# Two graph-attention layers of a four-layer GNN kernel: another order of the pipeline stages on three engines

## The chip, the cores and the metric

The kernel runs on one core of one Trainium2 chip, in one launch. The time is the device time of that core in microseconds (us); the median of three runs is given, and beside it the time of the one execution that the profiler recorded. The engines are TensorE (PE, its weight loads PEld), VectorE (DVE), ScalarE (ACT), GpSimd (POOL) and SyncE (SP, which only issues DMAs).

## The reference

Four graph layers run one after the other over 100,000 nodes with 64 features and 50,000 edges sorted by target node. Each adds its result to the node features after a layer norm and a ReLU. The first layer is a GATv2 attention with 8 heads of 16 features (followed by a second one with 2 heads of 64), the fourth a GATv2 attention with 4 heads of 16. Per edge both compute:

```python
z = leaky_relu(xl[src] + xr[dst] + ee, 0.2)
score = einsum('ehc,hc->eh', z, att)
m = segment_max(score, dst)
a = exp(score - m[dst])
alpha = a / (segment_sum(a, dst)[dst] + 1e-16)
out = segment_sum(xl[src] * alpha[..., None], dst)
```

The fourth layer also needs the mean and the variance of `out` over the nodes. The other layers are not touched by the change.

## The kernel before

`program` calls one block for each part of the work, and between two blocks all engines meet at a barrier. `gat_block` is called three times: with tag "a" (first attention, R=128 rows, 8 heads), "b" (wide, R=128, 2 heads) and "g" (last attention, R=64, 4 heads). The change touches the tags "a" and "g", the first and the third call. Tiles carry the tag in front (`a_xg`, `g_xg`).

A block works through 98 chunks of 512 edges, and each engine has its own list of stages. A stage is a function for one chunk. The helper `flow` runs step t of an engine as: for each entry (lag, stage) of the list, in the order of the list, run the stage for chunk t minus lag. So the list sets two things: the order of the work on an engine within a step, and how many steps after its gather a chunk meets the stage. Chunks go round four sets of buffers (SL = 4), and semaphores count chunks, so an engine waits only where the data of a chunk, or a buffer, isn't there yet. After a few steps written out, `flow` on DVE, PE and SP (and on ACT for "b" and "g") is a hardware loop whose body holds four steps. POOL's list is written out in full.

The stages, with the lines that are named later:

- POOL `gather` (line 802): eight indirect DMAs for each chunk, 128 rows each, with the row numbers read from `c_at` in SBUF. It waits first until the chunk four before has been normed and stored.
- DVE `norm`: in "g" an addition of two SBUF tiles first (830), then eight row statistics (649) and twelve small steps (661 to 675). `leaky` (850) takes the maximum of z and 0.2 z, the second operand from PSUM. `quotients`: a reciprocal (890) and the product with PSUM (905, in "g" 912). `denominator` (869, "a" only): a running sum along the edges over `ex`, both operands in SBUF. `sums`: the weights times features (879, both operands in SBUF), then the running sum (882, operands in SBUF). `maximum`: a small copy (858), a running maximum with scores from PSUM (859), a subtraction with PSUM (860).
- ACT: `normed` (938, in "a" two copies of node numbers more, 945 and 946; in "g" two stores, 950 and 951), `turned` (959, PSUM to SBUF), `values` (975, 0.2 z), `features` (968), `exponents` (983, 984, 986), `results` (stores the chunk; in "g" also a square, 992).
- PE: `turn` (1035, four transposes of the normed rows), `project` ("a" 1052 to 1054, "g" 1049 and 1050), `scores` (1060), `results` (1069, 1071 for "a": the running sums transposed), `moments` (1076, "g" only).

The chain of one chunk is gather, norm, normed, turn, turned, project, values, leaky, scores, maximum, exponents, sums and denominator, results on PE, quotients, results on ACT, moments.

Of the kernel before, what the change touches and what calls it, by code (L numbers as in the profile page):

```python
# [64 lines left out]
def hold(eng, turn, *waits):  # L65


    for sem, value in waits:
        eng.wait_ge(sem, value)
        eng.sem_inc(turn, 1)  # L70
# [52 lines left out]
def flow(eng, stages, total=NCH, slots=2, looped=True, alike=None):  # L123

    stages = [(s[0], s[1], total if len(s) < 3 else s[2]) for s in stages]
    lag = max(s for s, _, _ in stages)
    first = -(-(lag + slots) // slots) * slots  # L130
    last = (alike or total) // slots * slots
    if not looped:
        first = last = total

    def step(t):
        for s, fn, chunks in stages:
            n = t - s
            if 0 <= n < chunks:
                fn(n, n % slots, n // slots, n >= slots)

    for t in range(first):
        step(t)
    if looped:
        with eng.Fori(first // slots, last // slots) as i:
            for u in range(slots):
                for s, fn, _ in stages:
                    n = i * slots + (u - s)
                    fn(n, (u - s) % slots, i + (u - s) // slots, True)
    for t in range(last, total + lag):
        step(t)  # L150


def later(n, least=1):

    return not isinstance(n, int) or n >= least
# [524 lines left out]
def gat_block(nc, a, T, C, tag, H, R, wide):  # L680
# [10 lines left out]
    with ExitStack() as ctx:  # L691
# [3 lines left out]
        L = 2 if wide else 3  # L695
# [14 lines left out]
        both = R < P  # L710
# [98 lines left out]
        def _(dve):  # L809
# [104 lines left out]
                                    ).then_inc(S["oE"], 1)  # L914
            if wide:
                stages = [(L, leaky), (L + 2, quotients), (L + 1, denominator), (L + 1, sums), (L, maximum)]
            else:
                stages = [(L, leaky), (L + 2, quotients), (L + 1, sums), (L, maximum), (L - 2, norm)]
                if not both:
                    stages.insert(2, (L + 1, denominator))  # L920
            flow(dve, stages, slots=SL)
            if tag == "g":
                dve.wait_ge(S["bs"], NCH)
# [4 lines left out]
        def _(act):  # L928
# [65 lines left out]
                act.dma_start(rows(T[{"a": "H1", "b": "HR"}[tag]], n), oE[k][:, :, :]).then_inc(s_st[k], 16)  # L994
            if wide:
                stages = [(L - 1, features), (L - 2, turned), (L, exponents), (L + 2, results)]
            else:
                stages = [(L, values), (L, features), (L - 1, normed), (L - 1, turned), (L, exponents), (L + 2, results)]
            flow(act, stages, slots=SL, looped=tag != "a")
            for k in slots:  # L1000
                act.wait_ge(s_st[k], 16 * chunks_of(k, SL))
# [14 lines left out]
        @block.tensor  # L1016
        def _(pe):
            mm, tr = nc.tensor.matmul, nc.tensor.transpose
            wz, we, att = ((C["wz1"], C["we1p"], C["att1r"]) if tag == "a" else
                           (None, C["we2p"], C["att2r"]) if tag == "b" else  # L1020
                           (C["wz3"], C["we3"], C["att3r"]))

            def turn(n, k, q, old):
                if wide:
                    pe.wait_ge(s_g[k], NG * (q + 1))
                else:
                    pe.wait_ge(S["hn"], n + 1)
                if later(n):
                    pe.wait_ge(S["h"], n)
                if wide:  # L1030
                    for j in range(J):
                        tr(split(bT2[:, :])[:, :, j], xg[k][:, j, 1, :], C["ident"][:, :])  # L1032
                for j in range(J):
                    src = xg[k][:, j, 0, :] if wide else hn[k][:, j, :, :].rearrange("p s d -> p (s d)")
                    last = tr(split(bT[:, :])[:, :, j], src, C["ident"][:, :])  # L1035
                last.then_inc(S["hT"], 1)

            def project(n, k, q, old):

                pe.wait_ge(s_ext[k], 16 * (q + 1))  # L1040
                pe.wait_ge(S["h"], n + 1)
                if later(n):
                    pe.wait_ge(S["zt"], n)
                    pe.wait_ge(S["xl"], n)
                wx, hx = (C["wl2"][:, :], hT[k][:, :]) if wide else (wz[0:D, :], hT[k][0:D, :])
                wr, hr = (C["wr2"][:, :], hT2[k][:, :]) if wide else (wz[:, :], hT[k][:, :])
                if tag == "g":

                    mm(bZ[:, :], C["wz3"][:, :], hr, start=True, stop=False)
                    mm(bZ[:, :], we[:, :], ext[k][:, :], start=False, stop=True).then_inc(S["z"], 1)  # L1050
                    return
                mm(bZ[0:R, :], wr, hr, start=True, stop=False)
                mm(bZ[0:R, :], we[:, :], ext[k][:, :], start=False, stop=True)
                mm(bX[0:R, :], wx, hx, start=True, stop=True).then_inc(S["z"], 1)

            def scores(n, k, q, old):
                hold(pe, S["pturn"], (S["zt"], n + 1))
                if later(n):
                    hold(pe, S["pturn"], (S["ed"], n))
                mm(bS[:, :], att[:, :], zt[k][:, :], start=True, stop=True).then_inc(S["s"], 1)  # L1060

            def results(n, k, q, old):
                hold(pe, S["pturn"], (S["sum"], n + 1))
                if not both:
                    hold(pe, S["pturn"], (S["den"], n + 1))
                if later(n):
                    hold(pe, S["pturn"], (S["oE"], n))
                for j in range(J):
                    last = tr(bO[:, j * P:(j + 1) * P], split(num[k][:, :])[:, :, j], C["ident"][:, :])
                    if not both:  # L1070
                        last = tr(bD[:, j * P:(j + 1) * P], split(den[k][:, :])[:, :, j], C["ident"][:, :])
                last.then_inc(S["o"], 1)
            def moments(n, k, q, old):
                hold(pe, S["pturn"], (S["sq"], n + 1), (s_em[k], 16 * (q + 1)))
                for j in range(J):
                    last = mm(bB[:, :], oE[k][:, j, :, :].rearrange("p s r -> p (s r)"), em[k][:, j:j + 1],
                              start=isinstance(n, int) and n == 0 and j == 0, stop=isinstance(n, int) and n == NCH - 1 and j == J - 1)
                last.then_inc(S["bs"], 1)
            if wide:
                stages = [(L, scores), (L - 1, project), (L - 2, turn), (L + 1, results)]  # L1080
            else:
                stages = [(L, project), (L, scores), (L - 1, turn), (L + 1, results)]
            if tag == "g":
                stages.append((L + 3, moments))
            flow(pe, stages, slots=SL)


# [1187 lines left out]
```

## Time and profile before

| what | value |
|---|---|
| median of 3 runs | 7306.34 us (7302.04 to 7308.86) |
| profiled execution, its own time | 7280.67 us |
| span of the profile | 7278.9 us |
| busy over the span: DVE, POOL, PE, ACT | 75%, 61%, 55%, 44% |
| "a": first gather starts, last gather starts, last DVE work ends | 654.6, 1716.8, 1751.6 us |
| "g": first gather starts, last gather starts, last DVE work on g_oE | 5561.5, 6600.0, 6630.9 us |
| mean granted TensorE clock | 0.721 of full speed |

Busy shares over the whole span mix twelve blocks with different limits. The two blocks of the change take about 1100 and 1075 us of the 7279, and are read by themselves. In the rows below "idle <-X" behind a group is the time in which the engine stood still before these instructions and what ended it; "issue" is a pause in which it waited for nothing that the profile shows.

### The profile page before, as it was taken

The page shows a single profiled execution, that of the slowest core. Times are in us where ns is not written, and L with a number is a line of the kernel's source. Part 1 is how long each engine was busy: PE and PEld are TensorE (multiplying, and loading weights), DVE is VectorE, ACT ScalarE, POOL GpSimd, SP SyncE. Part 2 cuts the span into 40 slices and gives each one's busy share as a digit, 9 for nine tenths or more (in the row PEclk, how much of TensorE's full clock was granted, in tenths as well). Part 3 has the DMA queues.
Part 4 walks back from the last instruction along what each step waited for, and adds up shares of the span by engine and source line. Part 5 has one row for each costly group of instructions (what it writes and reads, how often), then busy time and mean ns, then how long its engine had stood idle before and what let it go on. Part 6 is the DMA issues. An engine that isn't in the chain of part 4 may idle for free. (4 is left out here: it accounts for less than half of the span.)

```text
span 7278.9 us, 83566 instructions
## 1 busy us (share of the span) xinstructions
PE 3968.5 (55%) x13024; PEld 2369.0 (33%) x13024; DVE 5486.2 (75%) x16937; ACT 3171.6 (44%) x7568; POOL 4455.4 (61%) x4321
## 2 busy tenths in 40 slices
PE   0002666664665665997000989876886766773000
PEld 0000332322333334886000545672332433331000
DVE  4502898986777777887777999776887888886886
ACT  0001666663333333776444000124554666665555
POOL 2777777775777776775776000007664777774776
PEclk9999677776888887555555989558997676665555
DMA  6001555555333332212998000459884555554554
GB/s 190 4 1 34 99 98 98 100 98 81 87 85 84 86 85 61 49 47 57 121 118 102 2 5 1 136 150 129 155 152 108 116 113 115 113 115 110 169 167 136
DMA packets 905930, 687.04 MB, mean 94 GB/s; under 512 B 595425, under 2 KB 744702, under 8 KB 905180
## 3 DMA queue, kind: packets, MB, share of 16 engines
q1 hardware_dynamic: 517168, 403.39, 20.5%
q0 software_dynamic: 137984, 138.92, 18.9%
q10 hardware_dynamic: 250600, 143.02, 6.5%
q14 instruction: 147, 1.20, 0.1%
q8 instruction: 31, 0.51, 0.0%
HBM read 491.06 MB, written 227.24 MB: 99 GB/s over the span
## 5 line engine op out<-in xcount | busy, mean ns | idle before, releaser
L1793 POOL DMA_INDIRECT f_dg<-t_D,c_at x392 | 379.7, 969 | 1132.5 <-POOLq L179 943.3
L802 POOL DMA_INDIRECT b_xg<-t_H,c_at x784 | 828.4, 1057 | 286.0 <-issue 238.6
L802 POOL DMA_INDIRECT g_xg<-t_D,c_at x784 | 801.7, 1023 | 319.9 <-issue 237.7
L802 POOL DMA_INDIRECT a_xg<-t_XL,c_at x784 | 824.6, 1052 | 250.1 <-issue 238.7
L2181 POOL DMA_INDIRECT out<-n_yo,c_at x392 | 430.8, 1099 | 237.5 <-issue 116.0
L440 POOL DMA_INDIRECT t_XL<-su_pos,su_scatx x392 | 388.2, 990 | 244.7 <-DMA t_XL<-in_nodes 125.7
L1326 POOL DMA_INDIRECT l_d<-t_D,l_ix x392 | 399.3, 1019 | 174.8 <-issue 115.8
L1141 POOL DMA_INDIRECT t_RANK<-m_place,m_at x392 | 400.8, 1022 | 160.9 <-issue 115.7
L938 ACT ACTIVATE a_hn<-a_xg,a_sm 128x64 f32<-128x64 f32 x784 | 269.9, 429 | 399.0 <-DVE a_sm L675 398.0
L1375 ACT ACTIVATE l_hn<-l_xs,l_sm 128x64 f32<-128x64 f32 x784 | 265.0, 426 | 284.0 <-DVE l_sm L675 218.9
L2160 ACT ACTIVATE n_h<-n_x,n_sm 128x64 f32<-128x64 f32 (+1 forms) x800 | 269.4, 426 | 210.0 <-DVE n_sm L675 210.0
L1915 ACT ACTIVATE f_hn<-f_xs,f_bykind 128x64 f32<-128x64 f32 x784 | 265.1, 426 | 178.9 <-DVE f_bykind L1825 178.9
L1032 PE MATMUL b_bank<-c_ident,b_xg 128*128 128x128 f32 x392 | 93.6, 383 | 415.4 <-DMA b_xg<-t_H,c_at 415.4
L1060 PE MATMUL a_bank<-a_zt,c_att1r 128*128 128x512 f32 x196 | 196.4, 1105 | 221.2 <-DVE a_zt L850 221.2
L1416 PE MATMUL pr_prow<-c_ident,pr_col 128*1 128x128 f32 x2 | 0.6, 395 | 567.0 <-DVE pr_col L1434 567.0
L1035 PE MATMUL a_bank<-c_ident,a_hn 128*128 128x128 f32 x392 | 108.4, 432 | 369.1 <-ACT a_hn L938 369.0
L938 ACT ACTIVATE g_hn<-g_xg,g_sm 128x64 f32<-128x64 f32 x784 | 269.6, 427 | 76.4 <-DVE g_sm L675 76.2
L1060 PE MATMUL g_bank<-g_zt,c_att3r 128*128 128x512 f32 x196 | 159.5, 907 | 258.2 <-DVE g_zt L850 258.2
L958 ACT ACTIVATE b_hT<-b_bank 128x512 f32<-128x512 f32 x98 | 58.5, 597 | 521.1 <-PE b_bank L1035 521.1
L1253 ACT ACTIVATE m_xn<-m_pa,m_sm 128x64 f32<-128x64 f32 x784 | 242.4, 414 | 90.5 <-DVE m_sm L675 89.1
L1704 ACT ACTIVATE e_ng<-e_pw 128x256 f32<-128x256 f32 x98 | 37.5, 383 | 535.2 <-PE e_pw L1695 535.2
L1495 PE MATMUL pb_sums<-pb_rhs,pb_lhs 128*128 128x392 f32 x784 | 260.6, 496 | 11.3 <-DVE pb_rhs L1486 11.3
(451 smaller groups left out, 13667.4 us busy)
## 6 DMA issues: line engine op xcount, KB each, us to landing
a_ends<-t_LAST SPq DMA_DIRECT2D x98, 256.0 KB
t_XSD<-a_xg SPq DMA_DIRECT2D x98, 256.0 KB
t_H<-a_oE ACTq DMA_DIRECT2D x98, 256.0 KB
b_ends<-t_LAST SPq DMA_DIRECT2D x98, 256.0 KB
l_xb<-t_XSD SPq DMA_DIRECT2D x49, 512.0 KB
f_rl<-t_REL SPq DMA_DIRECT2D x49, 512.0 KB
g_xb<-t_XSD SPq DMA_DIRECT2D x98, 256.0 KB
g_ends<-t_LAST SPq DMA_DIRECT2D x98, 256.0 KB
```

The source lines that it names most:

```text
L440: nc.gpsimd.indirect_dma_start(lp, bass.IndirectOffsetOnAxis(ap=scatx[:, f:f + 1], axis=0), pos[:, f:f + 1].bitcast(F32), None, bounds_che ...
L802: nc.gpsimd.indirect_dma_start(xg[k][:, j, i, :], None, table, bass.IndirectOffsetOnAxis(ap=C["at"][:, i, n * J + j:n * J + j + 1], axis=0 ...
L938: last = f(hn[k][:, g // 2, g % 2, :], xg[k][:, g // 2, g % 2, 0:D], ACT.Relu, bias=sm[:, 5, g:g + 1], scale=sm[:, 4, g:g + 1])
L1060: mm(bS[:, :], att[:, :], zt[k][:, :], start=True, stop=True).then_inc(S["s"], 1)
L1141: nc.gpsimd.indirect_dma_start(rank, bass.IndirectOffsetOnAxis(ap=at[k][:, j:j + 1], axis=0), place[k][:, j:j + 1], None).then_inc(s_rank[ ...
L1326: nc.gpsimd.indirect_dma_start(d1[k][:, 0, j, :], None, T["D1"], bass.IndirectOffsetOnAxis(ap=ix[k][:, j:j + 1], axis=0)).then_inc(s_g[k], 16)
L1375: last = nc.scalar.activation(hn[k][:, g % 2, g // 2, :], xs[k][:, g // 2, g % 2, :], ACT.Relu, bias=sm[:, 5, g:g + 1], scale=sm[:, 4, g:g ...
L1495: nc.tensor.matmul(sums[:, :], lhs[c % SL][:, :], rhs[c % SL][:, :], start=(c == 0), stop=(c == EF - 1)).then_inc(s_mm, 1)
L1793: nc.gpsimd.indirect_dma_start(dg[k][:, u, j, :], None, T["D2"], bass.IndirectOffsetOnAxis(ap=C["at"][:, 0, (2 * n + u) * J + j:(2 * n + u ...
L1915: last = f(hn[k][:, g // J, g % J, c, :], xs[k][:, g // J, g % J, :], ACT.Relu, bias=by_kind[:, c, 1, g:g + 1], scale=by_kind[:, c, 0, g:g ...
L2160: last = f(h[k][0:np_, g, :], x[k][0:np_, g, :], ACT.Relu, bias=sm[0:np_, 5, g:g + 1], scale=sm[0:np_, 4, g:g + 1])
L2181: nc.gpsimd.indirect_dma_start(out, bass.IndirectOffsetOnAxis(ap=C["at"][:, 0, j:j + 1], axis=0), yo[:, j, :], None, bounds_check=N - 1, o ...
```

## The change

The lists of stages for "a" and "g" get another order, and some lags change. No instruction is added, removed or given another size; "b" keeps its lists.

```diff
 # DVE
+            elif tag == "a":
+                stages = [(4, denominator), (3, leaky), (4, sums), (5, quotients), (3, maximum), (1, norm)]
             else:
-                stages = [(L, leaky), (L + 2, quotients), (L + 1, sums), (L, maximum), (L - 2, norm)]
-                if not both:
-                    stages.insert(2, (L + 1, denominator))
+                stages = [(1, norm), (3, leaky), (5, quotients), (4, sums), (3, maximum)]
 # ACT
+            elif tag == "a":
+                stages = [(3, values), (2, normed), (3, features), (2, turned), (3, exponents), (5, results)]
             else:
-                stages = [(L, values), (L, features), (L - 1, normed), (L - 1, turned), (L, exponents), (L + 2, results)]
+                stages = [(3, values), (3, features), (2, turned), (1, normed), (3, exponents), (6, results)]
 # PE
+            elif tag == "a":
+                stages = [(3, project), (5, results), (3, scores), (2, turn)]
             else:
-                stages = [(L, project), (L, scores), (L - 1, turn), (L + 1, results)]
-            if tag == "g":
-                stages.append((L + 3, moments))
+                stages = [(2, turn), (7, moments), (3, scores), (2, project), (4, results)]
```

L is 3 for both tags. In "a" the lags of DVE stay as they were, `denominator` goes from just ahead of `sums` to the head of the step, and `leaky` and `sums` follow it ahead of `quotients`; PE's `results` goes from the end of the step (lag 4) to between `project` and `scores` (lag 5). In "g" DVE's `norm` goes from the end of a step to its head; ACT takes `normed` one step sooner and behind `turned`, and stores one step later; PE takes `project` one step sooner and behind `scores`, and `moments` one step later.

## Rows read from the trace of the kernel before

**Rows 1.** Groups on POOL in the two blocks: busy us, mean ns, idle before

```profile
L802 POOL DMA_INDIRECT a_xg<-t_XL,c_at x784 | 824.6, 1052 | 250.1 <-issue 238.7 <-POOLq L179 11.5
L802 POOL DMA_INDIRECT g_xg<-t_D,c_at x784 | 801.7, 1023 | 319.9 <-issue 237.7 <-POOLq L179 81.3 <-DMA t_HN<-g_hn 0.9
```

**Rows 2.** Tile a_xg: ns min/median/max, first and last start

```profile
L802 POOL DMA_INDIRECT a_xg<-t_XL,c_at x784: 940/944/1781, 654.6 to 1716.8; - x196
```

**Rows 3.** Waits of DVE, 700 to 1700 us and 5620 to 6580 us: total, times, longest

```profile
DVE a_zt L850 <- ACT a_zt L975: 38.2, 39, 1.8
DVE a_bn L649 <- DMA a_xg<-t_XL,c_at: 9.3, 35, 1.4
...
DVE g_xg L830 <- DMA g_xg<-t_D,c_at: 75.3, 83, 1.6
```

**Rows 4.** Timeline of POOL in "a" around 1005 us: start, duration

```profile
999.57 1.60 POOL L802 DMA_INDIRECT a_xg<-t_XL,c_at  x1 [0.30 <-issue]
...
1008.97 0.94 POOL L802 DMA_INDIRECT a_xg<-t_XL,c_at  x1 [0.30 <-issue]
1010.22 1.55 POOL L802 DMA_INDIRECT a_xg<-t_XL,c_at  x1 [0.30 <-issue]
```

**Rows 5.** Timeline of DVE over the same time

```profile
1002.64 1.11 DVE L649 BATCH_NORM_STATS2 a_bn<-a_xg 128x6 f32<-128x64 f32 x8
...
1006.10 0.68 DVE L850 TENSOR_TENSOR a_zt<-a_zt,a_bank 128x512 f32<-128x512 f32 x1
1006.70 0.35 DVE L890 RECIPROCAL a_recT<-a_bank 128x32 f32<-128x32 f32 x1
...
1007.79 1.27 DVE L869 TENSOR_TENSOR_SCAN a_den<-a_ex,a_den 128x512 f32<-128x512 f32 x1
1008.98 0.71 DVE L879 TENSOR_TENSOR a_msg<-a_ex,a_xl 128x512 f32<-128x512 f32 x1
1009.73 1.28 DVE L882 TENSOR_TENSOR_SCAN a_num<-a_ex,a_num,a_msg 128x512 f32<-128x512 f32 x1
...
1012.41 0.69 DVE L860 TENSOR_TENSOR a_ed<-a_bank,a_r 128x512 f32<-128x512 f32 x1
```

**Rows 6.** Timeline of DVE in "a", a step with the loop's turn in it

```profile
1035.21 0.69 DVE L860 TENSOR_TENSOR a_ed<-a_bank,a_r 128x512 f32<-128x512 f32 x1
1035.82 1.10 DVE L649 BATCH_NORM_STATS2 a_bn<-a_xg 128x6 f32<-128x64 f32 x8
...
1039.59 0.69 DVE L850 TENSOR_TENSOR a_zt<-a_zt,a_bank 128x512 f32<-128x512 f32 x1 [0.33 <-issue]
```

**Rows 7.** Timeline of POOL and DVE in "g" around 5890 us

```profile
5886.65 1.43 POOL L802 DMA_INDIRECT g_xg<-t_D,c_at  x1 [0.30 <-issue]
...
5893.37 1.89 POOL L802 DMA_INDIRECT g_xg<-t_D,c_at  x1 [0.30 <-issue]
...
5886.57 0.69 DVE L830 TENSOR_TENSOR g_xg<-g_xg,g_xb 128x512 f32<-128x512 f32 x1 [1.39 <-DMA g_xg<-t_D,c_at]
...
5892.43 0.67 DVE L879 TENSOR_TENSOR g_ex<-g_ex,g_xl 64x512 f32<-64x512 f32 x1
5893.23 1.28 DVE L882 TENSOR_TENSOR_SCAN g_num<-g_ex,g_num 128x512 f32<-128x512 f32 x1
```

**Rows 8.** Timeline of all engines in "a", 1209 to 1217 us

```profile
1209.29 0.69 DVE L860 TENSOR_TENSOR a_ed<-a_bank,a_r 128x512 f32<-128x512 f32 x1
...
1210.65 1.12 PE L1054 MATMUL a_bank<-a_hT,c_wz 64*128 64x512 f32 x2
...
1211.20 1.06 ACT L986 ACTIVATE a_ex<-a_gap 128x1024 f32<-128x1024 f32 x1
...
1214.64 2.05 PE L1060 MATMUL a_bank<-a_zt,c_att1r 128*128 128x512 f32 x2 [2.87 <-DVE a_zt L850]
```

**Rows 9.** Timeline of the end of "g": the last chunk's addition and its quotients

```profile
6603.71 0.69 DVE L830 TENSOR_TENSOR g_xg<-g_xg,g_xb 128x512 f32<-128x512 f32 x1 [0.51 <-DMA g_xg<-t_D,c_at]
...
6630.88 0.42 DVE L912 TENSOR_TENSOR g_oE<-g_bank,g_recT 128x256 f32<-128x256 f32 x1
```

## The prediction

> **What bounds the kernel now.** I read first the groups on POOL in each of the two blocks. In both, POOL issues 784 gathers, and outside the wait at the start of the block nothing but a fixed pause stands between them: 238.7 us over 783 pauses, 0.305 us each, put down to "issue" [rows 1]. It is hardly ever held back by its own waits (0.9 us in all of "g"). So the end of a block is set by the rate of the gathers. The median gather takes 0.944 us [rows 2]; with the pause that is 1.248 us, and eight make 9.98 us for a chunk. But the first and the last gather of "a" lie 1062.2 us apart [rows 2], over 783 steps 1.357 us, or 10.85 us for a chunk. The mean gather is 1.052 us, not 0.944 [rows 1]: 0.87 us a chunk are lost in stretched gathers (85 us over the block). In "g" the mean is 1.023: 0.63 us a chunk, 62 us in all, and 10.61 us for a chunk.
>
> Next I laid the timelines of POOL and DVE side by side to see what stretches a gather. In "a" the gather that starts at 1010.22 takes 1.55 us and ends at 1011.77 [rows 4]. It began 0.49 us into the running sum of line 882, which ends at 1011.01 [rows 5], so it ends 0.76 us behind that. In "g" the gather at 5893.37 begins 0.14 us into the same sum, takes 1.89 us and ends 0.75 us behind it; the one at 5886.65 begins 0.08 us into the addition of line 830 and ends 0.82 us behind it [rows 7]. The gather at 1008.97 starts 0.01 us ahead of the product of line 879 and takes its normal 0.94 us [rows 4, 5]. All the long gathers of both blocks fit one rule, where "two SBUF operands" are lines 830, 869, 879 and 882: a gather that starts from about 0.1 us after the start of such an instruction is held until that instruction is over, and ends 0.75 us (running sum) or 0.82 us (product, addition) behind it. As an undisturbed one takes 0.944, starts later than 1.09 us into a running sum (1.28 + 0.75 - 0.944), or 0.55 us into a product, cost nothing. The running maximum of line 859, with one operand in PSUM, stretches none.
>
> The Trainium skill, SBUF — State Buffer, section Who interferes with whom, has a GpSimd instruction and a DVE instruction with two SBUF inputs share a port, with whichever starts first holding it for its whole length; it adds, as inferred only, that a tensor_tensor takes the reading side while descriptor generation needs the writing side, so that it wouldn't hold up a DMA's issue. The trace speaks against that addition: the addition of line 830 holds a gather by 0.49 us. By that addition lines 830 and 879 would cost nothing and the sum for "g" would lose one of its two causes; I go by the rows.
>
> Last I asked how far DVE is from being the bound. In "a" it waits for a gather's landing only 35 times in 92 chunks, 9.3 us in all, and 38.2 us for ACT's `values` ahead of `leaky`; in "g" it waits for the landing in 83 of about 90 chunks, 75.3 us [rows 3]. Without any wait a step of DVE in "a" is: norm 3.46 (1002.64 to 1006.10), leaky 0.60, reciprocal and product 1.09, line 869 1.19, product 0.75, line 882 to the start of 860 2.68 [rows 5], and from 860 to the next norm 0.61 [rows 6]: 10.38 us. The same sum with the shorter gaps seen elsewhere in the block is some 10.2. One step in four holds the turn of the loop, which shows ahead of the first stage of a list: norm to `leaky` is then 3.77 and not 3.3 to 3.5 [rows 6], +0.1 us a chunk. So DVE needs about 10.35 us, more than POOL's undisturbed 9.98 and less than the 10.85 that it takes. "a" is bound by POOL, and by how often DVE's stages catch its gathers.
>
> **"a": the new order, walked through.** No work goes; the cost of every moved instruction is unchanged, and the DMAs that ACT and SP issue are the same in number. What changes is the distance between DVE's three instructions that catch gathers.
>
> Before, 869, 879 and 882 follow each other at 0, 1.19 and 1.94 us [rows 5]. A gather caught by 869 is released at 1.27, ends at 2.03, and the next starts at 2.33: 0.39 into 882, held 0.70 us more. So each catch costs twice, u plus 0.7, where u is what remained of 869.
>
> After, 869 is at 0, `leaky` at 1.19, the product at 1.79 and the sum of 882 at about 2.5. The gather behind a caught one again starts at 2.33: 0.54 into the product, where the window has just closed; it costs 0.01. Released or not, the next starts at 3.58, 1.09 into the running sum, where the window has closed too. The second catch is gone, and with it 0.7 us of the chunks that had it. A gather that starts between 1.09 and 1.25 us into 869 costs nothing at all.
>
> Now the steady state has two forms. **Form 1, DVE waits for the landing.** A chunk's last gather ends at E (1001.17 [rows 4]) and norm starts at E + 1.47 [rows 5]; line 869 follows 3.43 later, E + 4.90. The gathers start at E + 0.30 plus multiples of 1.248: one at 5.29, caught 0.39 in, held 0.70. The period is 9.98 + 0.70 + 0.01 = 10.69, longer than DVE's own, so DVE waits again. **Form 2, DVE doesn't wait.** If POOL is ahead, each period shifts the phase by the difference until the catch equals it: the period is DVE's 10.35, and POOL is held 0.3 to 0.4 a chunk. It holds itself there. The way from 1 to 2 is a step in which 869 starts later than E + 5.2, so that the gather at 5.29 isn't caught. The turn of the loop now lies just ahead of 869: norm to 869 is 3.77 there, 1.47 + 3.77 = 5.24. Such a step is free of catches, POOL takes 9.98 and DVE 10.7, and DVE is behind by more than a landing from then on. As there are 21 such steps, I take form 2 to come within the first third of the loop at the latest, and most likely by chunk 15. There is no way back in the walk.
>
> The sum for "a": 15 chunks at about 10.7 against 10.85, 2 us; 83 at 10.35 against 10.85, 42 us: **-44 us**. With DVE's step at 10.2 it is -57; with 30 chunks in form 1, -38.
>
> What covers the moved stages: times from 869's start, PE at the lower of its two clock levels (1.2 of 2.4 GHz). `leaky` ends at 1.9; scores take 2.05 [rows 8], 4.0; the running maximum wants them at 4.85, 0.85 us of slack. 860 ends at 7.5; exponents take 2.28 (1209.98 to 1212.26 [rows 8]), 9.8; 869 wants them at 10.35, 0.55 of slack: that is the tightest. `project` (its last matmuls end at 1211.77, as the exponents do [rows 8]) now starts right behind `turned`, no later than before, and `values` some 1.5 us ahead of need; PE's `results` runs in the idle time ahead of scores, 2.87 us [rows 8]. ACT takes `normed` ahead of `features`, whose output is read one step later.
>
> **"g": the same order of DVE in another phase.** Read round the step, DVE's list is norm, leaky, quotients, sums, maximum before and after; only the chunk numbers differ, and the loop's turn moves from between norm and `leaky` to ahead of norm, where DVE waits for the landing anyway. DVE's step is about 9.5 us, less than 9.98, so it is always in form 1, and always catches by 830 and by 879 or 882. Added up from the timeline, over the chunks of before in which `leaky` followed norm without a wait (47 of them, all with the addition at E + 1.4 to 1.75) the gathers were held 0.70 us a chunk, and over the steady part of the block 0.69. A later `leaky` costs nothing on average: sometimes it slips the sums out of a gather's way. So the rate stays: **+1 us**, and from both sides -15 (0.55 a chunk, the best of the four places in the loop) to +15 (0.85, landings under 1.6 us).
>
> The tail of "g" gets longer. The last chunk's addition starts at 6603.71 and its quotients at 6630.88, 27.2 us later [rows 9]. With norm at the head of its step, the stages of that step (5.3 us) lie between the last norm and the next `leaky`, not ahead of it: **+5 us**, from 0 to +8. The tail of "a" keeps its lags on DVE: 0, to +2.
>
> Sum: -44 + 1 + 5 = **-38 us** against the profiled execution's own time, 7280.7 to 7242.7. The median of the runs is 25.7 us above the profiled execution; the difference is carried over: 7306.3 - 38 = **7268 us**. A measurement of this kernel can tell about 0.2%, 14.6 us, from no change.
>
> **Rivals.**
>
> *A. "a" stays in form 1.* If the landings come at E + 1.35 to 1.4, the loop's turn isn't enough to escape. Then three steps in four take 10.69 and the fourth about 11.0: 10.77, -8 us; with +6 for "g", 7304 us. For it: the margin at the turn is 0.03 to 0.05 us. Against it: landings differ from chunk to chunk by 0.1 us and more, and one escape is enough.
>
> *B. Slower: `leaky` waits in "a".* If `values` comes late by W, the product and the sum move away from 869 by W while the gathers stay where they are, and the period of form 1 is 10.70 + W. From W = 0.16 the gain is gone, from 0.3 the kernel is slower by 14 us, and at 1.0 the gather at 3.58 is caught at the start of the running sum for 1.0 as well: 11.7 a chunk, +83 + 6 us, 7395. For it: 38.2 us of this wait before, up to 1.8 us. Against it: before, `project` stood behind `results` that waited for this step's sums; now it doesn't.
>
> *C. "a" gains all.* DVE's step at its shortest and "g" at the better bound: -57 - 15 + 5 = -67, 7239 us.
>
> *D. "g" catches worse* (0.85 a chunk) while "a" is in form 1: +15 + 5 - 8 = +12, 7318 us, just inside of what can't be told.
>
> **Chances.** Form 2 in "a" 0.62 (of it C at 0.08), A 0.20, D 0.06, B 0.10; the last 0.02 is left for faster in another way. Of form 2 nearly all is more than 0.2% faster; A and D lie within 0.2% for the most part, and a fifth of them beyond it on either side: faster 0.65, same 0.21, slower 0.14. The likeliest case alone spans 7250 to 7286. The range for 8 in 10 takes in C and A: 7238 to 7312.
>
> **What would show it.** Right: the mean gather of "a" falls from 1.052 to about 0.99 us and the last gather starts near 1672; DVE's wait for the landing in "a" is gone, and so is the wait for `values`; long gathers of about 1.6 us that follow another long one are gone. The mean gather of "g" stays at 1.01 to 1.04. Wrong: a mean gather of about 1.03 in "a" with DVE waiting for the landing in nearly all chunks (A); a wait ahead of 850 or of 869 in "a" (B); a mean gather in "g" far from 1.02, which would mean that the phase there depends on something that I left out. The sum is most open where the windows end within 0.05 us of a start.

## The result, and the profile after

The changed kernel takes 7215.8 us in the median of 4 runs (7215.6 to 7224.4), the kernel before 7307.6 us in 4 runs beside it. The ratio is 0.9877, with a 95% interval of 0.986 to 0.9894: about 90 us faster. Forecast were 38 us and 7268, in a range of 7238 to 7312. The direction was right; the time lies 22 us below the range.

The profiled execution has a span of 7222.6 us. The groups on POOL, the tiles and the waits of DVE, for [rows 1 to 3]:

```profile
L802 POOL DMA_INDIRECT a_xg<-t_XL,c_at x784 | 771.7, 984 | 250.2 <-issue 238.8 <-POOLq L179 11.5
L802 POOL DMA_INDIRECT g_xg<-t_D,c_at x784 | 772.8, 986 | 319.8 <-issue 238.5 <-POOLq L179 81.0 <-DMA t_HN<-g_hn 0.3
```

```profile
L802 POOL DMA_INDIRECT a_xg<-t_XL,c_at x784: 941/947/1826, 657.6 to 1667.1; - x196
L802 POOL DMA_INDIRECT g_xg<-t_D,c_at x784: 941/947/1880, 5528.7 to 6539.3; - x196
```

```profile
DVE a_den L869 <- issue: 10.8, 22, 0.6
DVE a_bn L649 <- DMA a_xg<-t_XL,c_at: 2.6, 6, 0.5
...
DVE g_xg L830 <- DMA g_xg<-t_D,c_at: 74.6, 88, 2.6
```

The reader is to see three things. The pauses between gathers are the same 239 us; the gathers are shorter in the mean, 0.984 us instead of 1.052 in "a" and 0.986 instead of 1.023 in "g". From the first gather to the last, "a" takes 1009.5 us instead of 1062.2 (10.31 a chunk), "g" 1010.6 instead of 1038.5 (10.33 a chunk). And DVE hardly waits any more in "a": 6 waits for a landing, 2.6 us in all, none for `values`; the 22 pauses ahead of 869 are the loop's turn. As whole blocks, "a" went from 1098.1 to 1043.5 us and "g" from 1075.0 to 1051.3: 78 us together. The other blocks of this one execution are some 22 us longer than in the profiled one of before. The change doesn't touch them; a second profile of the kernel before (below) moves single ones of them by up to 6 us, so it is at least in part the spread of single executions. So the two profiled executions differ by 56 us and the medians by 92: the profiled one of before lies 27 us below the median of its kernel, and the profiled one of after 9 us above its own.

### The profile page after: what moved, and what is told of

Same layout as the page of the kernel before. It is cut to its first block and busy times, and to the rows that moved or that the text cites. A ratio compares the mean times of both kernels' runs of the same rounds, so it can differ in the third digit from the quotient of the medians.

```text
span 7222.6 us, 83578 instructions
## 1 busy us (share of the span) xinstructions
PE 3989.2 (55%) x13024; PEld 2366.8 (33%) x13024; DVE 5466.3 (76%) x16937; ACT 3174.0 (44%) x7568; POOL 4374.6 (61%) x4321
## 5 line engine op out<-in xcount | busy, mean ns | idle before, releaser
L802 POOL DMA_INDIRECT g_xg<-t_D,c_at x784 | 772.8, 986 | 319.8 <-issue 238.5
L802 POOL DMA_INDIRECT a_xg<-t_XL,c_at x784 | 771.7, 984 | 250.2 <-issue 238.8
L1062 PE MATMUL g_bank<-g_zt,c_att3r 128*128 128x512 f32 x196 | 194.0, 1091 | 202.8 <-DVE g_zt L850 202.6
```

The lines of the kernel that those rows point to most:

```text
L802: nc.gpsimd.indirect_dma_start(xg[k][:, j, i, :], None, table, bass.IndirectOffsetOnAxis(ap=C["at"][:, i, n * J + j:n * J + j + 1], axis=0 ...
```

## What the new order does in "a", row by row

POOL and DVE in "a" of the changed kernel, one step in which 869 catches a gather:

```profile
1107.71 0.95 POOL L802 DMA_INDIRECT a_xg<-t_XL,c_at  x1 [0.30 <-issue]
1108.96 1.59 POOL L802 DMA_INDIRECT a_xg<-t_XL,c_at  x1 [0.30 <-issue]
1110.85 0.95 POOL L802 DMA_INDIRECT a_xg<-t_XL,c_at  x1 [0.30 <-issue]
1112.10 0.95 POOL L802 DMA_INDIRECT a_xg<-t_XL,c_at  x1 [0.30 <-issue]
```

```profile
1108.51 1.28 DVE L869 TENSOR_TENSOR_SCAN a_den<-a_ex,a_den 128x512 f32<-128x512 f32 x1 [0.51 <-issue]
1109.71 0.66 DVE L850 TENSOR_TENSOR a_zt<-a_zt,a_bank 128x512 f32<-128x512 f32 x1
1110.29 0.68 DVE L879 TENSOR_TENSOR a_msg<-a_ex,a_xl 128x512 f32<-128x512 f32 x1
1111.01 1.28 DVE L882 TENSOR_TENSOR_SCAN a_num<-a_ex,a_num,a_msg 128x512 f32<-128x512 f32 x1
1112.21 0.33 DVE L890 RECIPROCAL a_recT<-a_bank 128x32 f32<-128x32 f32 x1
```

The gather at 1108.96 starts 0.45 us into the running sum of 869, ends at 1110.55, 0.76 behind the sum's end. The next one starts 0.56 us into the product of 879, and the one after it 1.09 us into the running sum of 882; both take 0.95. That is the walk of the prediction to 0.02 us: the second catch is gone. The timelines of the whole block say the same. In the 82 chunks from chunk 12 to 93 (counted from 0), the kernel before has 57 gathers held by 869, and the next gather is held again in all 57 cases; the changed kernel has 82 held gathers, one in each chunk, all by 869, and none is followed by a second.

Added up from this timeline, norm starts 2.23 to 2.35 us behind a chunk's last gather from chunk 11 on, in every chunk up to the end (before it jumped between 1.4 to 1.6 and 3.1 to 3.2). This is form 2 of the prediction: DVE doesn't wait and POOL's catches fill the difference. The chunks go by in a cycle of four, held 0.24, 0.09, 0.64 and 0.23 us; the 0.64 is the loop's turn. DVE's steps in this cycle are 10.1, 10.1, 10.7 and 10.2 us, 10.30 in the mean. In the 950 us of the waits above, the pauses that the profile lists on DVE add up to 13.6 us, 10.8 of them the loop's turn.

## The experiments

**1. Each block alone, and the kernel before again.** The first keeps the old lists of "g", the second the old lists of "a", the third is the kernel before.

```diff
 # a_only: "g" on DVE, ACT and PE
-                stages = [(1, norm), (3, leaky), (5, quotients), (4, sums), (3, maximum)]
+                stages = [(L, leaky), (L + 2, quotients), (L + 1, sums), (L, maximum), (L - 2, norm)]
...
 # g_only: "a" on DVE, ACT and PE
-                stages = [(4, denominator), (3, leaky), (4, sums), (5, quotients), (3, maximum), (1, norm)]
+                stages = [(L, leaky), (L + 2, quotients), (L + 1, denominator), (L + 1, sums), (L, maximum), (L - 2, norm)]
...
```

> The new lists for "a" alone, "g" as before. Theory 1 (the gain in "a" is the second catch that is gone, and DVE sets the period): the mean gather of a_xg falls to 0.98 us, the period is 10.3 us, the gathers of g_xg stay at a mean of 1.02; the whole is 50 to 60 us faster than before, ratio 0.992 to 0.993. Rival (most of the time came from elsewhere, since the runs differ by 92 us and the profiled blocks of "a" and "g" by 78): the ratio is further from 1 than 0.991 or nearer than 0.995.

> The new lists for "g" alone. If the two blocks add up and the profile's 24 us for "g" is all of it: ratio 0.996 to 0.997. If the step at which my sum failed is "g" and is larger in most executions than in the profiled one: ratio 0.994 to 0.995, and the two ratios of this call together give the 0.988 of the whole change. If what "g" gained is a chance of how "a" ended (a phase carried over), g_xg is back at a mean gather of 1.02 and the ratio is 1.0.

> The kernel before once more, for a second profile of it. If the profiled execution of before was a quick one (it lies 26 us under the median of its runs), this one is some 20 us longer, and the comparison by blocks shows where: either in "a" and "g" (the catches fall worse in most executions), or in blocks that the change doesn't touch.

Measured: "a" alone 7221.8 us, ratio 0.9917 (0.9903 to 0.993); "g" alone 7250.3 us, ratio 0.9961 (0.9948 to 0.9975); the kernel before 7282.4 us on that chip. The two shortfalls, 0.0083 and 0.0039, add up to 0.0122, against 0.0123 for the whole change: within the intervals, which leave some 0.0025 (18 us) open, the two blocks add up. The profiles give 55 us for block "a" of the first (1043.3 us) and 27 us for block "g" of the second (1047.6), against 61 and 32 us by the medians; the rest of each lies in blocks that the change doesn't touch and isn't explained. The second profile of before has a span of 7279.3 us, within 0.4 us of the first, with mean gathers of 1.054 and 1.023, and its kernel's median on this chip is 7282: the profiled execution of before was not an odd one, and my guess that it was quick is wrong. The median of the first runs was 7308; on which chip they ran is not on record. Groups of a_only and of g_only:

```profile
L802 POOL DMA_INDIRECT a_xg<-t_XL,c_at x784 | 771.6, 984 | 250.2 <-issue 238.7 <-POOLq L179 11.5
L802 POOL DMA_INDIRECT g_xg<-t_D,c_at x784 | 805.6, 1028 | 319.7 <-issue 238.7 <-POOLq L179 80.9
```

```profile
L802 POOL DMA_INDIRECT a_xg<-t_XL,c_at x784 | 827.2, 1055 | 250.1 <-issue 238.7 <-POOLq L179 11.5
L802 POOL DMA_INDIRECT g_xg<-t_D,c_at x784 | 768.0, 980 | 319.8 <-issue 238.3 <-POOLq L179 81.2 <-DMA t_HN<-g_hn 0.3
```

**2. "a": DVE's list or PE's?** Both are the changed kernel with a part of "a" taken back.

```diff
 # a_dve_only: PE and ACT in "a" as before
-                stages = [(3, values), (2, normed), (3, features), (2, turned), (3, exponents), (5, results)]
+                stages = [(L, values), (L, features), (L - 1, normed), (L - 1, turned), (L, exponents), (L + 2, results)]
...
-                stages = [(3, project), (5, results), (3, scores), (2, turn)]
+                stages = [(L, project), (L, scores), (L - 1, turn), (L + 1, results)]
...
 # a_pe_act_only: DVE in "a" as before
-                stages = [(4, denominator), (3, leaky), (4, sums), (5, quotients), (3, maximum), (1, norm)]
+                stages = [(L, leaky), (L + 2, quotients), (L + 1, denominator), (L + 1, sums), (L, maximum), (L - 2, norm)]
```

> The changed kernel with the old lists of PE and ACT in "a"; only DVE's order is new there. If the distance between DVE's catching instructions makes the gain in "a" (the walk finds values in time with the old lists too): mean gather of a_xg 0.98 to 0.99, period 10.3 us, time that of the changed kernel within 8 us. If the gain comes from PE's results between project and scores, which ends leaky's wait: mean gather above 1.03, 40 us or more slower than the changed kernel.

> The changed kernel with the old list of DVE in "a": 869, 879 and 882 stand together again, PE and ACT have the new lists. By the walk leaky no longer waits, but each catch by 869 is followed by a second one of 0.7 us: period 10.5 to 10.75 us, mean gather 1.01 to 1.04, 20 to 45 us slower than the changed kernel. If PE's order makes the gain: period 10.3.

Measured: with DVE's list alone 7200.0 us, ratio 0.9875 (0.9859 to 0.9892), block "a" 1042.9 us against 1043.5 in the changed kernel; with PE's and ACT's alone 7230.3 us, ratio 0.9915 (0.9898 to 0.9931), block "a" 1075.6. The same group in the two, DVE's list alone first, and DVE's wait for a landing with PE's and ACT's lists alone:

```profile
L802 POOL DMA_INDIRECT a_xg<-t_XL,c_at x784 | 772.0, 985 | 250.1 <-issue 238.6 <-POOLq L179 11.5
```

```profile
L802 POOL DMA_INDIRECT a_xg<-t_XL,c_at x784 | 804.4, 1026 | 250.1 <-issue 238.6 <-POOLq L179 11.5
```

```profile
DVE a_bn L649 <- DMA a_xg<-t_XL,c_at: 15.1, 66, 1.9
```

The order of DVE alone makes the whole gain in "a". The new lists of PE and ACT add nothing to it. By themselves they take 22 us off the block, and `leaky` no longer waits for `values`; the period is then 10.65 us, with DVE waiting for a landing in 66 chunks, form 1, and three chunks in four held 0.5 to 0.6. Here each gather held by 869 is again followed by a second held one (22 of 22 from chunk 12 to 93). The walk gave 10.5 to 10.75.

**3. "g": the later load?** In the changed kernel SP issues the load of `g_xb`, which norm also needs, 3 to 6 us ahead of the end of the chunk's last gather, before 17 to 21 us ahead of it: its queue waits in `masks` for `moments`, which comes a step later. Norm starts 1.8 us behind the last gather in the median, before 1.6.

```diff
-                flow(sp, [(0, stored), (1, extras), (1, segment_ends), (2, masks)], slots=SL)
+                flow(sp, [(0, stored), (1, extras), (1, segment_ends), (5, masks)], slots=SL)
```

> The changed kernel, with SP's masks of "g" at lag 5 instead of 2, so that the load of g_xb no longer stands behind a wait for moments. Theory X ("g" gained because the load of g_xb now lands later than the gathers, so that norm starts at 1.8 and not 1.6 us behind them and its catches fall elsewhere): g_xb is issued 15 us or more ahead of the last gather's end again, norm is back at 1.55 to 1.65 us, the mean gather goes from 0.986 back to 1.01 to 1.03 us and the kernel is 18 to 35 us slower than the changed one (ratio to before 0.991 to 0.993). Rival Y (it gained because leaky no longer waits for values, whatever the load does): the mean gather stays at 0.98 to 0.99 and the ratio at 0.988.

Measured: 7204.0 us, ratio 0.9893 (0.9878 to 0.9909), which overlaps the changed kernel's 0.9877; block "g" 1055.3 us, norm at 1.65, mean gather 0.990. The four other profiles with the new lists of "g" have 1047.6 to 1051.6 us, so the late load is worth 4 to 8 us of the block at most, not the 24, and the spread between single executions is half of that. Theory X (the later load made the gain) falls.

**4. "g": leaky's wait for values.** The kernel before, with `project` one step sooner and behind `scores` and `turn` on PE, and then with the early load as well.

```diff
 # on the kernel before, both
+                if tag == "g":
+                    stages = [(3, scores), (2, turn), (2, project), (4, results)]
 # g_sooner_free also
-                flow(sp, [(0, stored), (1, extras), (1, segment_ends), (2, masks)], slots=SL)
+                flow(sp, [(0, stored), (1, extras), (1, segment_ends), (5, masks)], slots=SL)
```

> The kernel before with one move in "g": PE runs project one step sooner, behind turn, so that values and leaky never wait for it; the lists of DVE, ACT and SP and the lag of moments are those of before, "a" is as before. Theory Y (the gain in "g" is that leaky always follows norm at once, which lets the phase settle where few gathers are caught): no wait ahead of 850, mean gather 0.98 to 0.995, "g" 15 to 28 us shorter (ratio 0.996 to 0.998). Rival (it takes norm at the head of the list, or the later load): mean gather stays at 1.01 or more, ratio within 0.001 of 1.

> The kernel before with PE's project one step sooner in "g" and SP's masks at lag 5, so that the load of g_xb is early again. If the later load is what costs the run with project sooner half of its gain (norm there starts 2.1 us behind the last gather in the median, scattered from 1.5 to 3.0): norm back at 1.6 to 1.7, mean gather 0.985 to 1.0. If it is the loop's turn between norm and leaky that costs it: mean gather stays at 1.00 to 1.02, and the chunks with the turn carry 0.6 us or more of held time, as they do with project sooner alone.

> As for this kernel before, on a chip of the usual speed: the kernel before with project sooner in "g" and the load of g_xb early. If the late load cost the run with project sooner half of its gain: norm at 1.6 to 1.7 behind the last gather, mean gather 0.985 to 1.0. If the loop's turn between norm and leaky does: mean gather 1.00 to 1.02, with 0.6 us or more held in the chunks with the turn.

Measured for the first: 7273.5 us, ratio 0.9981 (0.997 to 0.9992); block "g" 1060.5 us against 1074.4 to 1077.7 with the old lists. Waits of DVE in "g", of the second profile of the kernel before and of this kernel:

```profile
DVE g_zt L850 <- ACT g_zt L975: 27.3, 29, 1.5
```

```profile
DVE g_xg L830 <- DMA g_xg<-t_D,c_at: 81.5, 77, 3.5
...
DVE g_zt L850 <- ACT g_zt L975: 0.6, 2, 0.3
```

```profile
L802 POOL DMA_INDIRECT g_xg<-t_D,c_at x784 | 789.9, 1008 | 319.8 <-issue 238.0 <-POOLq L179 81.2 <-DMA t_HN<-g_hn 0.6
```

The wait ahead of 850 is gone, and the mean gather falls to 1.008, about 40% of the way from 1.023 to 0.986. Theory Y (the gain is that `leaky` no longer waits) had asked for 0.98 to 0.995: it holds in part. What is left is not this wait. Two things stand out, and which of them costs what is open. The gathers are held longest, 0.68 us, behind a norm with the loop's turn between it and `leaky`; and norm starts 2.35 us behind the last gather in the median, scattered from 1.4 to 3.95, though SP issues the load of `g_xb` 12 to 18 us ahead of that gather's end. The second kernel, meant to part these two, ran only on chips on which nothing of this can be read (next).

**5. Chips on which the kernel before takes 8450 to 8570 us.** The chips above, on which it takes 7280 to 7310 us, are called usual here. All further runs, the second kernel of experiment 4 among them, fell on four such chips. They are the changed kernel itself, and on top of it: one with DVE's order of "g" changed once more, one with 0.33 us more work on DVE in each chunk of "a" (into a tile of its own that nobody reads), and one with the idea of "a" applied to "b":

```diff
 # g_sums_first
-                stages = [(1, norm), (3, leaky), (5, quotients), (4, sums), (3, maximum)]
+                stages = [(1, norm), (4, sums), (3, leaky), (5, quotients), (3, maximum)]
 # a_more_dve2, in quotients (with the tile `spare` set up elsewhere)
+                if tag == "a":
+                    v.reciprocal(spare[:, :, :], weights)
 # b_split
-                stages = [(L, leaky), (L + 2, quotients), (L + 1, denominator), (L + 1, sums), (L, maximum)]
+                stages = [(L + 1, denominator), (L, leaky), (L + 1, sums), (L + 2, quotients), (L, maximum)]
```

> The changed kernel itself, on the chip of the run beside it. On a chip of the usual speed: ratio 0.987 to 0.989, as before. On a slow one, where "a" took 1370 us with the lists of before and 1450 to 1460 with the new ones: ratio 1.005 to 1.012, that is, the new order is slower there, because it leaves less time between a late step and POOL's wait for the chunk four before. Rival: if the slow chip's "a" differed by chance, 0.990 to 1.0.

> The changed kernel with DVE's list of "g" in the order norm, sums, leaky, quotients, maximum. By the rule the product now starts 4.05 us behind the start of norm, 5.7 to 5.9 us behind the last gather; the gathers that start at 5.29 and 6.54 then both miss the product's window (0.1 to 0.55 us into it) and the running sum's (0.1 to 1.09 into it, 6.45 to 7.65): mean gather 0.950 to 0.965, period 10.0 to 10.15 us, 15 to 30 us faster than the changed kernel. If the rule is only roughly right, the mean gather stays at 0.98 or more.

> As for this kernel before, on a chip of the usual speed: DVE's list of "g" in the order norm, sums, leaky, quotients, maximum. By the rule of the catches: mean gather of g_xg 0.950 to 0.965, period 10.0 to 10.15 us, ratio 0.984 to 0.986. If the rule is only roughly right: 0.98 or more, ratio 0.988.

> The changed kernel with DVE's list of "g" in the order norm, sums, leaky, quotients, maximum, a third time. On a chip of the usual speed, by the rule of the catches: product 5.7 to 5.9 us behind the last gather, the gathers at 5.29 and 6.54 miss both windows, mean gather of g_xg 0.950 to 0.965, period 10.0 to 10.15 us, 15 to 30 us faster than the changed kernel beside it. If the rule is only roughly right: mean gather 0.98 or more, no faster. On a slow chip, where late landings bound the block, nothing follows for the rule.

> The changed kernel with one reciprocal more for each chunk on DVE in "a" (the work of line 890 done once more into a tile that nobody reads, 0.36 us). If DVE's own step sets the period of "a" now: it goes from 10.3 to about 10.65 us, DVE still doesn't wait for a landing, and the kernel is 30 to 36 us slower than the changed one. If POOL still sets it: under 8 us.

> The same kernel as the run before with one reciprocal more on DVE in "a" (0.36 us a chunk), once more on a chip on which the kernel before takes 7280 to 7310 us, since the last one took 8542 and bounds "a" by late landings. If DVE's own step sets the period of "a": 10.3 goes to about 10.65 us, 30 to 36 us slower than the changed kernel (ratio 0.992 to 0.993). If POOL sets it: ratio 0.988.

> The changed kernel with one reciprocal more on DVE in "a" (0.36 us a chunk), a third time, as the last two times fell on chips on which the kernel before takes 8450 to 8540 us. On a chip of the usual speed: if DVE's own step sets the period of "a", it goes from 10.3 to about 10.65 us and the ratio is 0.992 to 0.993; if POOL sets it, 0.988.

> The changed kernel with DVE's list of "b" in the order denominator, leaky, sums, quotients, maximum, lags as they were. If the rule of the catches holds in "b" too, where a catch by 869 is followed by one of 882 in nearly every chunk (mean gather 1.057 us): mean gather 0.97 to 1.0, "b" 35 to 60 us shorter, ratio to before 0.980 to 0.984. If the chain through PE, for which DVE waits 226 us in "b", gets longer because quotients stands behind sums: "b" gets no shorter, ratio 0.988 or more.

> As for this kernel before, on a chip of the usual speed: DVE's list of "b" in the order denominator, leaky, sums, quotients, maximum. The last chip showed POOL waiting for PE's turn in "b" (140 us), which speaks for the longer chain. If the catches decide: mean gather of b_xg under 1.0, ratio 0.980 to 0.984. If the chain decides: ratio above 0.990.

| kernel | ratio to before on the same chip (95%) |
|---|---|
| changed kernel | 1.0108 (1.0085 to 1.0131) |
| g_sums_first | 1.0039 (1.0025 to 1.0053), 1.006 (1.003 to 1.009), 1.005 (1.0028 to 1.0072) |
| a_more_dve2, _r, _s | 1.0099, 1.0131, 1.0112 (intervals of 0.0024 to 0.0045 on either side) |
| b_split, _r | 1.0228 (1.0204 to 1.0252), 1.026 (1.0215 to 1.0306) |
| g_sooner_free, _r | 0.9992 (0.9963 to 1.0021), 1.0031 (1.0005 to 1.0057) |

So on the one such chip on which it was timed the changed kernel is 1.1% slower than before, and with the added work on DVE it is 1.0 to 1.3% slower on the three others. The profiles show where: "a" takes 1461.8 us with the new lists there (1429 to 1480 in the eight other profiles with them) and 1369.2 and 1360.8 us with the old ones (in the two runs of g_sooner_free); "g" takes 1493.1 with the new lists. But blocks that the change doesn't touch are longer as well: the block after "b" takes 777.5 us, and 573.4 in the first profile of the changed kernel. POOL's waits in "a", of g_sooner_free_r and then of the changed kernel there, in the same 1100 us:

```profile
POOL a_xg L802 <- issue: 222.1, 621, 2.1
POOL a_xg L802 <- ACT c_at L946: 206.7, 34, 8.3
```

```profile
POOL a_xg L802 <- ACT c_at L946: 299.2, 37, 11.8
POOL a_xg L802 <- issue: 214.1, 578, 8.4
```

Here POOL is held by its wait for the chunk four before, which doesn't occur on the usual chips, and more so with the new lists. It runs ahead and is not the bound any more: in the median of "a" norm starts 35 us behind its chunk's last gather (32 with the old lists), not 2.3, and in these 1100 us DVE never waits for a landing. Some of the expectations above say that late landings bound the block on such a chip; by these rows they don't. Nor do the catches come back: the mean gather of "a" is 0.965 to 0.974 us with the new lists and 1.013 and 1.019 with the old ones. Behind POOL's wait are pauses of ACT and DVE in which the trace shows neither an engine nor a DMA that ended them ("remote"): on ACT in the changed kernel,

```profile
1001.06 0.60 ACT L959 ACTIVATE a_hT<-a_bank 128x512 f32<-128x512 f32 x1 [5.32 <-remote]
...
1009.74 0.60 ACT L975 ACTIVATE a_zt<-a_bank 128x512 f32<-128x512 f32 x1 [5.96 <-remote]
...
1034.77 0.60 ACT L959 ACTIVATE a_hT<-a_bank 128x512 f32<-128x512 f32 x1 [8.82 <-remote]
```

What makes these pauses, and why they cost more with the new lists, is open. The added work on DVE costs nothing that can be seen here: block "a" takes 1450.9 and 1435.6 us with it, and 1455.6 to 1459.9 and 1429.4 to 1432.3 in the other profiles of the new lists on the same two chips. So DVE's step isn't the bound of "a" on such a chip. That it is on a usual one rests on the profile, in which DVE hardly stands still; the test for which that kernel was made was not measured there. b_split is 1.2 to 1.3% slower than the changed kernel with the added work on the same chip, with POOL waiting 140 and 151 us for PE's `turn` in "b", and was measured on these chips only. g_sums_first is 0.6% quicker than the changed kernel on the same chip (8606 to 8655 us) and still slower than the kernel before. No version was shown to beat both kernels on either sort of chip, but a_dve_only is level with the changed one on the usual sort.

## Why the prediction was right or wrong, point by point

- *POOL's gathers set both blocks, and DVE's instructions with two SBUF operands stretch them:* right. The pauses stayed at 239 us, only the gathers' mean moved, and the rows of "a" after meet the windows to 0.02 us.
- *"a", -44 us:* right in mechanism, small in size. Measured is -52.7 us from first to last gather, -54.6 for the block. Form 2 came at chunk 10 or 11, not 15, and DVE's step is 10.30 in the mean with the loop's turn in it (three of 10.1 to 10.2, one of 10.7); I had taken 10.35 from a step with the longer gaps, while the sum of the shorter ones stood beside it. Rivals A and B did not occur; experiment 2 shows that PE's part of the change, and with it rival B's wait, doesn't matter next to DVE's.
- *"g", +1 us at the rate:* this is the step that failed. Measured is -27.9 us from first to last gather, beyond the bound of -15 as well. The sentence under it, that DVE in "g" always catches a gather, was not even so before: 10 of 82 chunks there have no held gather. I took the held time of those chunks of before in which `leaky` hadn't waited, 0.70 us, for that of a kernel in which it never waits. In the steady part of "g" (82 chunks, from chunk 10 on) the held time falls from 55 to 23 us in all, 0.67 to 0.28 a chunk: 10 chunks have no held gather before, 39 after, the gathers held by 830 go from 28 to 6, and those by 882 from 33 us to 14. My reading is that the chunks that I had counted stood among others that had waited, and started from phases that these had left; experiment 4 bears it out in part only. The timeline of POOL and DVE in "g" of the changed kernel shows how near the edge it runs; the first gather starts 0.06 us into the running sum of 882 and passes, the second 0.39 us into the product of 879 and is held 0.15:

```profile
6003.33 0.95 POOL L802 DMA_INDIRECT g_xg<-t_D,c_at  x1 [0.30 <-issue]
...
6013.33 1.10 POOL L802 DMA_INDIRECT g_xg<-t_D,c_at  x1 [0.30 <-issue]
...
6003.27 1.32 DVE L882 TENSOR_TENSOR_SCAN g_num<-g_ex,g_num 128x512 f32<-128x512 f32 x1
...
6012.94 0.67 DVE L879 TENSOR_TENSOR g_ex<-g_ex,g_xl 64x512 f32<-64x512 f32 x1
```

- *The rest of "g":* with `project` sooner, and so without the wait for `values`, some 40% of it comes (experiment 4), and experiment 3 shows that the late load is behind little. By the timelines this 40% is the fall at 882, 33 to 18 us; the gathers held by 830 stay at 29 there, and fall only with the whole change, with the early load too. What remains of the change are norm at the head of DVE's list, with the loop's turn now ahead of it, and the moves of `normed`, `turned`, `turn`, `moments` and the stores on ACT and PE. Which of them makes the rest was not shown.
- *The tail of "g", +5 us:* right. From the end of the last gather to the last quotients 29.4 us before, 34.6 after. The tail of "a", forecast at 0 to +2, is 1.7 us shorter (33.7 and 32.0).
- *The median against the profiled execution:* the offset of 25.7 us that I carried over is no property of the kernel: on the chip of experiment 1 median and profile of before agree to 3 us, and in the changed kernel the profiled execution is 9 us above the median. A difference between two chips would explain it; that isn't shown. Of the 52 us between the forecast and the measured time, 40 are the two blocks, which gave 78 us and not 38; the other 12 lie in this offset and in blocks that the change doesn't touch, and aren't explained.
- Rival C (7239 us), all of "a" and a better "g", was nearest; its "g" was still 13 us too careful. I gave it 0.08. It was near by its size and not by its reason, as it held that "g" can't fall below 0.55 us a chunk. With the size of "g" open on both sides by its own phase, it deserved as much as A.

## What to carry to other kernels

Where one engine issues transfers back to back and another's instructions hold it up now and then, look at where within the period they fall, not at how busy either is: here the same instructions with 0.6 us of other work between them cost less than half as much (0.32 us a chunk, not 0.87). Such a phase settled by itself in "a", and in "g" a mean taken over some chunks of the old kernel (0.70 us held) was not that of the new order (0.28), even though those chunks looked alike; walk the new cycle until it repeats, or leave the size open. And an order that gains where one engine is the bound can lose on a chip on which another is: time it on more than one chip.

## What the runs showed that was not expected

- The held gather ends 0.75 to 0.76 us behind a running sum and 0.81 to 0.83 behind a product or addition of DVE, wherever in it it started: so do all of the some 2000 held gathers of "a" and "g" in the nine profiles on the usual chips. A start up to 0.08 us into a running sum and up to 0.04 into the addition passed.
- The gather behind a held one doesn't catch up: the pause stays 0.30 us, so a hold moves all that follow, and can lift them over the next window.
- The same kernel took 7282 us on one chip, 7308 in the first runs, and 8449 to 8568 us on four others, there with pauses of up to 12 us on ACT and DVE in "a"; the order that is 1.2% faster in the first runs is 1.1% slower on one of the four.
